# Mask products on GpSimd, another place for the residual's ones, and halved evictions at unit boundaries

## The reference

```
x: (128, 128, 512)   cond_8: (128, 8)   weight: (8, 512, 512)   mask: (512, 512)   bias: (512,)
masked_w = weight * mask[None, :, :]                    # (g, o, t)
w_bot    = einsum('bg,got->bot', cond_8, masked_w)      # one 512x512 matrix for each batch b
out      = x + einsum('bnt,bot->bno', x, w_bot) + bias
```

## Time and profile before

| | us |
|---|---|
| median of 3 runs (627.38 to 627.58) | 627.52 |
| the profiled execution's own time | 628.11 |
| its span, first to last instruction | 626.1 |
| TensorE busy in the span | 605.0 (97%) |
| VectorE busy | 262.1 (42%) |
| ScalarE busy | 144.0 (23%) |
| GpSimd busy | 0.2 (0%) |
| matmuls of the groups (2048 records) | 457.1 |
| fp32 matmuls of the bursts (4096 records) | 151.1 |
| matmuls of the ones (512 records) | 30.8 |

### The profile page before, as it was taken

One profiled execution on the slowest core, in us unless ns is written; L12 is line 12 of the kernel. 1 busy time (PEld: TensorE's weight loads), 2 busy tenths in 40 slices (PEclk: granted clock), 3 DMA queues, 4 the chain that ended last, 5 costly groups with the idle time before them and its releaser, 6 DMA issues.

```text
span 626.1 us, 15098 instructions
## 1 busy us (share of the span) xinstructions
PE 605.0 (97%) x6663; PEld 522.7 (83%) x6663; DVE 262.1 (42%) x409; ACT 144.0 (23%) x265; POOL 0.2 (0%) x4
## 2 busy tenths in 40 slices
PE   5879999999999999999999999999999999998997
PEld 3768888888888888888888888888888888887886
DVE  3853443443443455545443444434443443442121
ACT  2752222222222222222222222222222222220000
POOL 0000000000000000000000000000000000000000
PEclk9999999999999999999999999999999999999999
DMA  8965455455455578877455455445455445455712
GB/s 296 407 236 191 144 182 181 140 176 194 143 180 183 193 256 274 290 270 259 147 173 197 135 174 196 143 169 195 145 174 192 142 175 191 151 174 184 216 67 84
DMA packets 42800, 119.23 MB, mean 190 GB/s; under 512 B 4848, under 2 KB 5360, under 8 KB 42736
## 3 DMA queue, kind: packets, MB, share of 16 engines
q1 hardware_dynamic: 23328, 83.90, 40.1%
q10 hardware_dynamic: 19408, 34.38, 14.9%
HBM read 84.71 MB, written 33.55 MB: 189 GB/s over the span
## 4 chain that ended last, share of the span: by engine, by line
PE 93%; DVE 3%; issue 2%; DMA 2%; SPq 0%; DVEq 0%
PE ps L313 72%; PE ps L289 19%; DMA xs<-in_mask 2%; DVE wbot L230 2%; PE ps L299 1%; DVE wm L225 1%; SPq L155 0%; SPq L161 0%; DVE staged L239 0%; DVEq L223 0%; DVEq L238 0%; DVEq L132 0%
## 5 line engine op out<-in xcount | busy, mean ns | idle before, releaser
L313 PE MATMUL ps<-wbot,xs 128*128 128x256 f32 x2048 | 457.1, 382 | 5.6 <-DVE wbot L230 5.6
L313 PEld LDWEIGHTS ps<-wbot,xs 128*128 128x128 f32 x2048 | 384.4, 190 | 63.4 <-issue 9.3
L230 DVE COPY wbot<-ps 128x512 f32<-128x512 f32 x248 | 160.1, 686 | 221.2 <-PE ps L313 193.7
L187 ACT ACTIVATE wbot<-ps 128x512 f32<-128x512 f32 x264 | 142.8, 595 | 419.7 <-PE ps L313 210.6
L289 PEld LDWEIGHTS ps<-y_sb,wm 32*128 32x128 f32 x4096 | 135.4, 191 | 32.8 <-issue 23.0
L289 PE MATMUL ps<-y_sb,wm 32*128 32x128 f32 x4096 | 151.1, 288 | 10.3 <-DVE wm L225 8.2
L239 DVE TENSOR_TENSOR staged<-ps,bias_sb 128x512 f32<-128x512 f32 x128 | 88.0, 687 | 129.3 <-PE ps L313 129.3
L299 PE MATMUL ps<-ones_sb,eye_sb 32*128 32x128 bf16 x512 | 30.8, 217 | 0.4 <-DMA ones_sb<-in_ones 0.4
L299 PEld LDWEIGHTS ps<-ones_sb,eye_sb 32*128 32x128 bf16 x512 | 15.1, 96 | 0.7 <-DMA ones_sb<-in_ones 0.7
L225 DVE TENSOR_TENSOR wm<-wm,xs 128x512 f32<-128x512 f32 x16 | 10.9, 684 | 10.0 <-DMA xs<-in_mask 10.0
L225 DVE TENSOR_TENSOR wm<-wm,mask_sb 128x512 f32<-128x512 f32 x16 | 10.3, 684 | 0.0
## 6 DMA issues: line engine op xcount, KB each, us to landing
xs<-in_x SPq DMA_DIRECT2D x128, 512.0 KB, 3.7
out<-staged ACTq DMA_DIRECT2D x128, 256.0 KB, 3.4
wm<-in_w SPq DMA_DIRECT2D x15, 512.0 KB, 5.9
mask_sb<-in_mask SPq DMA_DIRECT2D x8, 512.0 KB, 4.8
xs<-in_mask SPq DMA_DIRECT2D x7, 512.0 KB, 12.7
wm<-in_w SPq DMA_DIRECT2D x2, 256.0 KB, 3.9
xs<-in_mask SPq DMA_DIRECT2D x2, 256.0 KB, 5.8
eye_sb<-in_eye ACTq DMA_DIRECT2D x1, 256.0 KB, 4.0
```

What stands on the lines that cost most here:

```text
L187: eng.activation(tile_place(b, j), tile_sums(b, j), ACT.Copy).then_inc(s_ev_a, 1)
L230: eng.tensor_copy(tile_place(b, j), tile_sums(b, j)).then_inc(s_ev_v, 1)
L313: ins = eng.matmul(bank[:, h * SL:(h + 1) * SL], xs[:, n % XRING, h, k, :], at, start=(k == 0), stop=(k == KT - 1))
```

## The change

GpSimd now makes the mask products, except the first two of slice 0, which stay on VectorE; each has a semaphore of its own, and all who waited for a product wait through `masked`. VectorE evicts tiles 1 and 3 in every burst. In odd bursts the ones for x come first, ahead of all fp32 matmuls, with block `own` behind them; in even bursts block `own` is the last of the fp32 matmuls and the ones come after it. The last burst of each unit is evicted in two halves of each tile: the half for groups 0 to 7 of all tiles, then the half for groups 8 to 15; group 0 of the unit waits for the first halves, group 8 for the second. The last group's two batches go into two banks, each with its own bias addition and store.

```diff
+TAKEN.append((2 * STEPS - 1, None))
...
-def on_vector(b, j):
-
-    return j == 3 or j == 1 and (b >= CS or b % 2 == 0)
+def on_vector(j):
+
+    return j % 2 == 1
+
+
+def pieces(b):
+
+
+    if b % CS < CS - 1:
+        return tuple((j, 0, GROUPS) for j in range(TILES))
+    return tuple((j, at, at + GROUPS // 2) for at in (0, GROUPS // 2) for j in range(TILES))
...
+        def tile_evicted(eng, b, j, end):
+            eng.wait_ge(s_ev_v if on_vector(j) else s_ev_a, DONE[b, j, end])
+
+        def masked(eng, s, c):
+
+            if s == 0 and c < BY_VECTOR:
+                eng.wait_ge(s_mul_v, c + 1)
+            else:
+                eng.wait_ge(s_mul_p, s * CS + c + 1 - BY_VECTOR)
...
+        @block.gpsimd
+        def _(eng):
+            for s in range(SLICES):
+                for c in range(CS):
+                    if s or c >= BY_VECTOR:
+                        multiply_mask(eng, s, c).then_inc(s_mul_p, 1)
...
-                eng.wait_ge(s_s2, n + 1)
...
+                if n < STEPS - 1:
+                    eng.wait_ge(s_s2, n + 1)
...
+                for h in range(GB):
+                    eng.wait_ge(s_s2, n + h + 1)
+                    eng.tensor_tensor(staged[:, n % OUTB, h * SL:(h + 1) * SL],
+                                      ps[BANK_OF[n + h * STEPS, None] % BANKS][:, 0:SL],
+                                      bias_sb[:, s * SL:(s + 1) * SL], ALU.add).then_inc(s_o, 1)
...
-                if n in MASK_AT:
-                    multiply_mask(1, MASK_AT[n])
-                    multiply_mask(1, MASK_AT[n] + 1)
...
-                    elif on_vector(b, j):
-                        eng.wait_ge(s_ev_v, V_DONE[b * TILES + j + 1])
                     else:
-                        eng.wait_ge(s_ev_a, A_DONE[b * TILES + j + 1])
+                        tile_evicted(eng, b, j, GROUPS)
...
+                ahead = b % 2 == 1
+                others = [k for k in range(KT) if k != own]
...
+                if ahead:
+                    add_x()
+                for k in [own] + others if ahead else others + [own]:
...
+                if not ahead:
+                    add_x()
...
+                if g in (0, GROUPS // 2):
+                    for j in range(TILES):
+                        tile_evicted(eng, (u + 1) * CS - 1, j, g + GROUPS // 2)
+                last = n == STEPS - 1
                 bank = room((n, None))
-                if g == 0:
-                    evicted(eng, (u + 1) * CS - 1)
```

More of the change, by code:

```diff
@@ L132, in tile_ready, with tile_place @@
                 eng.wait_ge(s_s2, b - CS + 1)
-        def tile_place(b, j):
+        def tile_place(b, j, first, end):
             u, c = divmod(b, CS)
@@ L166, in load_x @@
                 elif n >= 2:
-                    eng.wait_ge(s_mul, (n - 1) * 2)
+                    masked(eng, 0, n * 2 - 3)
                 u, g = divmod(n, GROUPS)
@@ L183, in _, with evict @@
         def _(eng):
[L184 to L187, removed]
+            def evict(b):
+                for j, first, end in pieces(b):
+                    if not on_vector(j):
+                        tile_ready(eng, b, j)
+                        eng.activation(tile_place(b, j, first, end), tile_sums(b, j, first, end),
+                                       ACT.Copy).then_inc(s_ev_a, 1)
             def store_out(n):
@@ L199, in _ @@
             for b in range(CS):
-                for j in range(TILES):
-                    evict(b, j)
+                evict(b)
             for n in range(STEPS):
                 for b in bursts_before(n):
-                    for j in range(TILES):
-                        evict(b, j)
+                    evict(b)
                     if n and b == bursts_before(n)[0]:
@@ L278, in burst, with add_x @@
                 own = s * SL // P + c * CO // P
+                rows = [slice(j * TR, (j + 1) * TR) for j in range(TILES)]
+                bank = [ps[BANK_OF[b, j] % BANKS] for j in range(TILES)]
+                ahead = b % 2 == 1
+                others = [k for k in range(KT) if k != own]
+                def add_x():
+                    if b == 0:
+                        eng.wait_ge(s_eye, 32)
+                    for j in range(TILES):
+                        if ahead:
+                            room((b, j))
+                        ins = eng.matmul(bank[j][:, own * P:(own + 1) * P], eye_sb[rows[j], c % (P // CO), :],
+                                         ones_sb[rows[j], :], start=ahead, stop=not ahead)
+                        if not ahead:
+                            ins.then_inc(s_s1, 1)
                 if b == 0:
@@ L283, in burst @@
                 if win == 0:
-                    eng.wait_ge(s_mul, s * CS + c + 1)
-                for k in range(KT):
+                    masked(eng, s, c)
+                if ahead:
+                    add_x()
+                for k in [own] + others if ahead else others + [own]:
                     for j in range(TILES):
[L287 to L291, removed]
-                            ins.then_inc(s_s1, 1)
[L293 to L302, removed]
+                        if not ahead and k == others[0]:
+                            room((b, j))
+                        ins = eng.matmul(bank[j][:, k * P:(k + 1) * P], wm[rows[j], c, k * P:(k + 1) * P],
+                                         y_sb[rows[j], win, :], start=not (ahead and k == own), stop=ahead or k != own)
+                        if ahead and k == others[-1]:
+                            ins.then_inc(s_s1, 1)
+                if not ahead:
+                    add_x()
             def group(n):
@@ L306, in group @@
                 eng.wait_ge(s_x[n % XRING], 16 * (n // XRING + 1))
+                if g in (0, GROUPS // 2):
+                    for j in range(TILES):
+                        tile_evicted(eng, (u + 1) * CS - 1, j, g + GROUPS // 2)
+                last = n == STEPS - 1
                 bank = room((n, None))
-                if g == 0:
-                    evicted(eng, (u + 1) * CS - 1)
                 for h in range(GB):
+                    if last and h:
+                        bank = room((n + h * STEPS, None))
+                    at_h = 0 if last else h * SL
                     for k in range(KT):
                         at = sums[:, g, :, k, h, :] if u % 2 else sums[:, :, g, k, h, :]
-                        ins = eng.matmul(bank[:, h * SL:(h + 1) * SL], xs[:, n % XRING, h, k, :], at,
+                        ins = eng.matmul(bank[:, at_h:at_h + SL], xs[:, n % XRING, h, k, :], at,
                                          start=(k == 0), stop=(k == KT - 1))
-                ins.then_inc(s_s2, 1)
+                    if last or h == GB - 1:
+                        ins.then_inc(s_s2, 1)
             eng.wait_ge(s_zeros, 1)
```

77 lines of the change are left out of this document (40 added, 37 removed).

## The result

| | before | changed |
|---|---|---|
| median, us | 627.55 (627.38 to 628.18, 4 runs) | 617.68 (615.86 to 618.64, 4 runs) |
| ratio | | 0.9837, 95% interval 0.9814 to 0.9861 |
| profiled execution, us | 628.11 | 615.86 |
| its span, us | 626.1 | 614.1 |

A second set of the changed kernel (e9) gave 616.24 (615.0 to 616.68), ratio 0.9807 (0.9785 to 0.983). The forecast was 620.9: faster, as predicted and within the range, but the gain of the medians is 9.9 us instead of 6.6, and between the two profiled spans it is 12.0.

The account below looks back on a forecast made before the run. TensorE, 93% of the chain of waits, was taken to bound the kernel; start 1.5, ones 1.8, boundaries 2.9 and tail 0.4 made 6.6 us off, 621.5 profiled and 620.9 as median. The range was 616.0 to 624.4.

Parts of the forecast that it names:

- Start: Before group 0: products leave VectorE, but instruction fetches then end last; group 0 at 40.0, gain 1.5 us, bounds 0 and 5.6.
- the second answer: Second instruction fetch in the start: 4.6 us from asking to ready, so ready at 26.1 us.
- Rival A: Start: fetches keep up and data binds; group 0 at 35.8, gain 5.6 instead of 1.5, total 616.8; chance 0.20.
- GpSimd's product: Slice 0: one mask multiplication on GpSimd taken at 1.2 us, bounds 0.69 and 2.7; last product at 33.2 us.
- rival C: Start: GpSimd's product so slow that it sets the start; at 2.7 us each, total 635.2; chance 0.08.
- Ones: Ordinary pairs of bursts: ones at the outer ends bring 33 cycles from 9.32 to 9.265 us, gain 1.8.
- Boundaries: Seven unit boundaries: evicting the last burst in halves and removing VectorE's products shorten stalls, gain 2.9 us, bounds 0.6 and 3.9.
- Two terms of 1.30 + 0.94 + 0.25 = 2.49: Boundary, from bursts' start to group: 1.30 to ScalarE's start, 0.94 its three pieces, 0.25 to the group; stall 0.33 remains.
- the boundary with slice-1 products: Boundary at 267.61: two products holding up VectorE leave, stall was 1.17 us, gain 0.9.
- Tail: After the last matmul: half a bias addition (about 0.42 us) and a 128 KB store; gain 0.4, bounds 0.2 and 0.9.

Follow-up runs that it names:

- e9: The changed kernel itself again, a second set with nothing altered; 616.24 us, ratio 0.9807.
- e5: Changed kernel with x late: the loads of x for groups 1 to 9 issued only when burst 15 is done; 612.24 us, ratio 0.9753.
- e2: Changed kernel with parity swapped: ones last in odd bursts, first in even ones, so both sets stand mid-pair; 623.41 us, ratio 0.9932.
- e12: Changed kernel with tile 0 of a unit's last burst evicted whole by ScalarE, the other three in halves; 617.87 us, one execution.
- e3: Changed kernel with the last burst of a unit evicted whole instead of in halves; 620.72 us, ratio 0.9889.
- e4: Changed kernel with all mask products on VectorE again and, in unit 0, tile 1 of odd bursts on ScalarE; 617.28 us, ratio 0.984.
- e1: Changed kernel with the ones for x back in their old place, behind block own wherever it stands; 622.95 us, ratio 0.9932.
- e6: Changed kernel with the first four products of slice 0 on VectorE instead of two; 617.53 us, ratio 0.984.
- e7: Changed kernel with 36 matmuls of 16 columns (72 instructions) added between bursts 0 and 1; 616.63 us, ratio 0.982.

## Why the prediction was right, and where it was not

**Start, forecast 1.5, measured 0.5, and -0.4 in the second profile.** The mechanism was right: the fetches that I read from four packets and two stalls are what ends last, now with three stalls, and x late removes them. The forecast group 0 of 40.0 was 1.0 early. The term that was mis-sized is the second answer. The first came as forecast (packet at 18.8, so usable by some 21.3, forecast 21.5). The second was forecast 4.6 later, at 26.1, and the first stall ended at 27.61; from there 6.2 and 6.5 us were as forecast (6.3, 6.7). The 4.6 hung on the moment of asking, 22.6, which no row shows; the packets themselves were already 6.3 apart in the kernel before (18.4 and 24.7), as they are here (18.8 and 25.2). I also read 0.65 us for a packet; the share is that of 16 engines, so it is 1.03 to 1.08, and the stalls end 1.4 behind a packet's end, not 1.9. The sum used the packet's start + 2.5, which stands: 2.4 in all three stalls here. Rival A (data-bound, group 0 at 35.8) did not come, but e5 nearly reached it with 37.10. The Trainium skill (Runtime: NRT & Kernel Launch, "Instruction fetch mechanics") calls fetching hidden; here it is hidden in the ordinary cycles, where TensorE has no wait for issue, and it is not while the bus is at a share of 1.03 and bursts take 1.3 us.

**GpSimd's product, taken at 1.2, is 1.27**, so rival C was far off. The last product ended at 34.0, not 33.2: the last four followed one another from 28.96 on without a wait, so the last pair started when GpSimd was free and not when its data landed. The estimate of 1.34 from the ratio 1.96 that the Trainium skill gives for 2048 columns (GPSIMD Engine Reference, "Elementwise — side-by-side cycle accounting") was close: the ratio to VectorE's 0.69 is 1.85.

**Ones, forecast 1.8, measured 6.5.** This is the term that failed. I read the two forms of cycle (9.32 and 9.27) as the number of turns and took "zero" for what no row showed, ones right behind a group, with 0.05 as its bound. e2 has the number of turns without the place and stays at 9.26: the place is worth 0.10 a cycle, twice my bound, over 49 cycles. The hint was in the trace of the kernel before (the four rows under e2): 32 fp32 matmuls behind a group take 1.10 and the next 32 take 0.95.

**Boundaries, forecast 2.9, measured 4.5.** The prices of the pieces were right (0.38 on ScalarE, 0.41 to 0.42 on VectorE, three on ScalarE 0.94). Two terms of 1.30 + 0.94 + 0.25 = 2.49 were too large. ScalarE started 1.21 behind the bursts' start instead of 1.30, since the burst is shorter, and the group started 0.15 behind ScalarE's third piece (113.47 + 0.94 = 114.41), not 0.25: 2.29 in all. VectorE's second piece (its four start 0.33 apart from 113.51 on) ends at 114.26, 0.29 before the group, and by the waits under e12 the group would have started only 0.03 earlier without the third piece. At the boundary with slice-1 products the gain was 1.16 (10.49 to 9.33), forecast 0.9. The experiments share out the 4.5: 3.5 for the halves (e3), 0.7 for those products (e4), and some 0.4 for the order of the ones (e1's seven gaps).

**Tail, forecast 0.4, measured 0.6**: the half addition takes 0.42 as forecast, and the smaller store 0.3 less.

**The total.** Against the forecast the start gave 1.0 us less, the ones 4.7 more, the boundaries 1.6 and the tail 0.2 more. The 12.0 between the profiled spans are more than the 11.5 that the range allowed; that the medians' 9.9 and 11.4 (e9) lie inside is partly luck.

## What to carry to other kernels

When an engine's idle time is called "issue", lay the instruction packets of the DMA table beside it: if the stalls end a fixed time behind packets (here 2.4 to 2.5 us) and the bus is full, a faster engine may bring nothing, as here, while holding back loads that nobody needs yet does (3.9 us from one added wait between the profiled spans, 4.0 to 5.4 between medians). Where matmuls of 32 rows follow matmuls of full height, try a few cheap ones first: here four bf16 ones saved 0.10 us each time. When several waits stand ahead of an instruction, look at which is met last: in e12 each wait behind that one took 0.11 us, though it had long been met. Moving the late one to the end was not tried. A price for a sequence that no row shows should be bounded by the largest difference seen between neighbours in the trace.

## What the runs showed of the hardware that was not expected

Some executions lose clock behind a stall. In e6, with stalls of 2.10, 0.86 and 1.86 us that end at 28.57, 34.85 and 41.33, the granted clock (eighth number) is at full speed, 2.4 GHz, for only part of these windows and at 1.2 for the rest:

```profile
30.00:38.00 8.00, 6.99 (x187) 6.54 (x184) 6.32 (x11) 5.62 (x11) 3.18 (x3) 0.83 1.03 408
...
42.00:46.00 4.00, 4.00 (x17) 3.19 (x12) 0.00 (x0) 0.00 (x0) 0.00 (x0) 0.62 0.03 9
```

Its first cycle took 10.85 us instead of 9.17. In e7 the window from 38 to 42 had 0.50 throughout, behind a stall of 2.17, and the first cycle took 10.32. The first profile of the changed kernel has stalls of 0.85, 1.65 and 1.86 and a full clock.

In the start itself the lower clock cost nothing. e9 and e12 run the same code up to the evictions of burst 15 and have nearly the same first long stall; behind it e9 lost clock and e12 did not (timeline row, then the window from 28 to 32, e9 first):

```profile
28.32 2.33 PE L343 MATMUL ps<-y_sb,wm 32*128 32x128 f32 x50 [1.88 <-issue]
```

```profile
28.00:32.00 4.00, 3.68 (x84) 3.68 (x88) 2.34 (x4) 2.17 (x4) 3.92 (x4) 0.66 1.03 410
```

```profile
28.45 1.72 PE L343 MATMUL ps<-y_sb,wm 32*128 32x128 f32 x50 [1.82 <-issue]
```

```profile
28.00:32.00 4.00, 3.49 (x102) 3.14 (x106) 2.63 (x5) 2.36 (x5) 3.93 (x4) 1.00 1.03 411
```

The next stall is 0.89 in e9 and 1.67 in e12, and it ends at 34.62 and 34.63, the last one at 41.10 in both, group 0 starts at 41.81 in both. The packets came at the same times in both (32.2 to 32.3 and 38.7 to 38.8), whatever the clock was. The lower clock costs where it reaches into group 0, as in e6 and e7.

The four runs of the changed kernel had mean clocks of 1.0, 0.983, 0.997 and 0.997 at 615.86, 618.64, 617.49 and 617.87 us. The clock alone does not order the times, though: e4's runs took 616.06 and 615.86 us at 0.992, and 618.5 and 618.6 at 0.997. e5, with one stall of 1.15, had 1.0 in three of four runs, which lie within 0.4 us. What decides whether a given stall is followed by the lower clock was not settled, nor how much of the runs' scatter is due to it.
